# An attention kernel on one core: scores in runs of three half tiles, and each query block's context split inside the tile loop

## What is computed

```python
scores = jnp.einsum('bqhd,bkd->bhqk', q, k) * scale        # 16 heads, one k of width 32
scores = jnp.where(causal, scores, min_val)
attn = jax.nn.softmax(scores, axis=-1)
ctx = jnp.einsum('bhqk,bkd->bqhd', attn, v)
out = jnp.einsum('bsd,ed->bse', ctx, out_w) + out_b
x = layernorm(x + out)
```

## Time and profile before

| | us |
|---|---|
| median of 3 runs | 1208.55 |
| lowest and highest of them | 1206.21, 1215.7 |
| the profiled execution | 1208.3 |
| its span, first to last instruction | 1206.1 |

### The profile page before, as it was taken

How to read it: one execution, slowest core, us unless ns; L and a number is a source line. 1 busy time by engine, 2 the same in 40 slices (tenths; PEclk the granted TensorE clock), 3 DMA queues, 4 the chain that set the end, 5 groups by cost and what they waited for, 6 DMA issues and landing times.

```text
span 1206.1 us, 18310 instructions
## 1 busy us (share of the span) xinstructions
PE 1102.0 (91%) x6056; PEld 529.5 (44%) x6080; DVE 896.4 (74%) x1095; ACT 712.2 (59%) x828; POOL 165.5 (14%) x153
## 2 busy tenths in 40 slices
PE   5499989998999999999988998999999899999986
PEld 4146433743335543333643743374333464333342
DVE  3176688769987689888677668865988757988856
ACT  4344568337884477886435346824788446788711
POOL 4220121102001011001013012020200101100000
PEclk9699999999999999999999999999999999999989
DMA  9911530064001550001153154016300135000000
GB/s 214 235 55 34 120 93 2 36 141 105 1 1 36 118 129 1 2 1 36 34 134 94 39 126 106 2 36 141 105 2 1 36 81 131 1 1 2 2 1 36
DMA packets 65678, 74.37 MB, mean 62 GB/s; under 512 B 14224, under 2 KB 48016, under 8 KB 65552
## 3 DMA queue, kind: packets, MB, share of 16 engines
q1 hardware_dynamic: 49968, 58.74, 19.2%
q0 software_dynamic: 13584, 11.54, 6.1%
q10 hardware_dynamic: 2000, 2.51, 0.7%
HBM read 25.58 MB, written 8.39 MB: 28 GB/s over the span
## 4 chain that ended last, share of the span: by engine, by line
PE 58%; DVE 25%; issue 8%; ACT 2%; POOL 2%; SPq 2%; DVEq 1%; DMA 1%; ACTq 0%; POOLq 0%
DVE psum_k L743 14%; PE sc L1053 13%; PE bank L1075 11%; PE sc L943 10%; PE sc L1192 7%; PE bank L943 7%; PE sc L1207 2%; DVE stats L819 2%; PE sc L1093 2%; DVE res L816 2%; SPq L364 2%; ACT prob L577 2%; PE bank L1093 2%; PE sc L1138 1%; POOL prob L467 1%
## 5 line engine op out<-in xcount | busy, mean ns | idle before, releaser
L577 ACT ACTIVATE prob<-sc 128x1024 f32<-128x1024 f32 x544 | 525.2, 1026 | 156.7 <-PE sc L1053 142.8
L743 DVE TENSOR_TENSOR psum_k<-psum_k,prob 128x2048 f32<-128x2048 f32 x170 | 395.6, 2327 | 5.1
L1053 PE MATMUL sc<-q_st,k_st 128*128 128x512 f32 x1088 | 334.3, 428 | 32.2 <-DMA q_st<-q_lo 16.3
L1053 PEld LDWEIGHTS sc<-q_st,k_st 128*128 128x128 f32 x1088 | 186.5, 191 | 279.8 <-ACT prob L577 180.2
L1075 PE MATMUL bank<-prob,v_sb 128*32 128x512 f32 x2176 | 289.1, 607 | 0.8 <-DVE ctxn L802 0.8
L467 POOL TENSOR_SCALAR_AFFINE_SELECT prob<-prob 128x1024 f32<-128x1024 f32 x64 | 88.0, 1419 | 605.6 <-ACT prob L577 605.5
L1192 PE MATMUL sc<-prob,w_sb 128*128 128x512 bf16 x488 | 117.9, 381 | 5.3 <-DVE prob L892 2.9
L743 DVE TENSOR_TENSOR psum_k<-prob 128x2048 f32<-128x2048 f32 x28 | 64.1, 2288 | 52.8 <-ACT prob L577 43.9
L1075 PEld LDWEIGHTS bank<-prob,v_sb 128*32 128x32 f32 x2176 | 43.8, 108 | 106.8 <-issue 89.9
L943 PE MATMUL bank<-q_st,wq_hi 128*128 128x512 f32 x240 | 81.0, 402 | 0.0
L609 ACT ACTIVATE prob<-sc 128x512 f32<-128x512 f32 x64 | 37.3, 597 | 68.1 <-PE sc L1192 68.0
(11 more groups left out here) (127 smaller groups left out, 998.6 us busy)
## 6 DMA issues: line engine op xcount, KB each, us to landing
q_st<-q_hi SPq DMA_DIRECT2D x128, 128.0 KB, 2.8
q_st<-q_lo SPq DMA_DIRECT2D x128, 128.0 KB, 2.8
res<-in_x SPq DMA_DIRECT2D x8, 1024.0 KB, 5.2
res<-ob_sb POOLq DMA_DIRECT2D x8, 1024.0 KB, 10.1
out_x<-res SPq DMA_DIRECT2D x32, 256.0 KB, 5.6
res<-in_xT SPq DMA_DIRECT2D x7, 1024.0 KB, 5.0
w_sb<-in_w POOLq DMA_DIRECT2D x8, 256.0 KB, 14.3
prob<-in_wqkvT ACTq DMA_DIRECT2D x4, 288.0 KB, 5.9
```

Of the source, the lines that this page charges most:

```text
L577: nc.scalar.activation(prob[t % NP][:, half * HW:(half + 1) * HW], score_half(q // TB, 2 * t + half).rearrange("p m n -> p (m n)"), ACT.Ex ...
L743: nc.vector.tensor_tensor(acc[:, :], first[:, :], prob[t % NP][:, :], ALU.add).then_inc(add_v, 1)
L1053: last = nc.tensor.matmul(dst, k_st[:, k * P:(k + 1) * P], q_st[slot][:, c * HJ:(c + 1) * HJ, at:at + P], start=True, stop=not shift)
```

## The change

The halves of the scores are no longer issued two at a time, tile by tile. A group's first two halves stand alone; after that they come in runs of three. A run is followed by the values of each tile that it has completed, alternately one tile and two, and by the denominators due at those tiles. `scored_by(g, u)` gives the tiles complete after half u, and is empty in the middle of a run. The ring's list of uses (`ring_of`) has the same new order, so denominators always stand between two runs.

The splits of the context move: the high part of block q is made on ACT after the exponential of tile `LAST[q] + 6`, the low part on DVE at tile `LAST[q] + 8`, where these tiles still belong to the group; otherwise behind the last tile, where all but the fourth block's now stand ahead of `split_high_x`. The number of instructions of each kind is as before.

```diff
+HIGH_LAG, LOW_LAG = 3, 5
+def split_at(q, lag):
+    t = LAST[q] + DLAG + lag
+    return t if t <= LAST[q // TB * TB + TB - 1] else None
+
+def halves_of(g):
+    return range(2 * FIRST[TB * g], 2 * LAST[TB * g + TB - 1] + 2)
+
+def scored_by(g, u):
+    first, last = halves_of(g)[0], halves_of(g)[-1]
+    if u == first + 1:
+        return [u // 2]
+    if u != last and (u - first - 1) % 3:
+        return []
+    begin = first + 2 + 3 * ((u - first - 2) // 3)
+    return range((begin + 1) // 2 if begin % 2 == 0 else begin // 2, (u + 1) // 2)
+
 def ring_of(g):
     uses = []
-    for t in range(FIRST[TB * g], LAST[TB * g + TB - 1] + 1):
-        uses += [("scores", 2 * t), ("scores", 2 * t + 1)]
-        uses += [("den", q) for q in denominators_at(t) if q >= TB * g]
+    for u in halves_of(g):
+        uses.append(("scores", u))
+        uses += [("den", q) for t in scored_by(g, u) for q in denominators_at(t) if q >= TB * g]
...
                         exp_tile(t)
-                        if t == t1 - 1:
-                            split_high_context(g, 0)
-                    split_high_context(g, 1)
+                        for n in range(TB):
+                            if split_at(TB * g + n, HIGH_LAG) == t:
+                                split_high_context(g, n)
+                    for n in range(TB - 1):
+                        if split_at(TB * g + n, HIGH_LAG) is None:
+                            split_high_context(g, n)
                     with if_more(act, b, g):
                         split_high_x(g + 1)
-                    split_high_context(g, 2)
                     split_high_context(g, TB - 1)
...
-                        if t > t1 - 2:
-                            split_low_context(g, t - t1 + 1)
+                        for n in range(TB):
+                            if split_at(TB * g + n, LOW_LAG) == t:
+                                split_low_context(g, n)
...
-                    for t in range(t0, t1 + 1):
-                        scores(t, g, shift)
-                        if t == t0 and g:
+                    for u in halves_of(g):
+                        scores(u, g, shift)
+                        if u == 2 * t0 + 1 and g:
                             finish_experts(g - 1)
-                        if t - LAG >= t0:
-                            times_values(PV_ORDER[t - LAG])
-                        for q in denominators_at(t):
-                            if q >= TB * g:
-                                denominators(q)
+                        for t in scored_by(g, u):
+                            if t - LAG >= t0:
+                                times_values(PV_ORDER[t - LAG])
+                            for q in denominators_at(t):
+                                if q >= TB * g:
+                                    denominators(q)
```

More of the change, by code:

```diff
@@ L927, in _ @@
                                 normalise_context(q)
-                    split_low_context(g, 2)
+                    for n in range(TB - 1):
+                        if split_at(TB * g + n, LOW_LAG) is None:
+                            split_low_context(g, n)
                     normalise_context(TB * (g + 1) - 1)
@@ L1035, in ring_free, with scores @@
                             pe.wait_ge(rden_ready, count(b, rden_ready, i + 1))
-                def scores(t, g, shift):
+                def scores(u, g, shift):
+                    t, half = divmod(u, 2)
                     q, k = TILES[t]
                     slot, at = (q % TB) // 2, (q % 2) * P
[L1040 to L1061, removed]
@@ new lines, in scores @@
+                    at_ring = RING_AT[g]["scores", u]
+                    ring_free(g, at_ring)
+                    if at_ring == 2:
+                        with pe.If(b > 0) if g == 0 else nullcontext():
+                            pe.wait_ge(resid2, count(b - (g == 0), resid2, TB * ((g - 1) % NG) + (2 if g else TB)))
+                            pe.sem_inc(waited_apart, 1)
+                    for m in range(2):
+                        c = 2 * half + m
+                        if t == FIRST[q] and q % 2 == 0:
+                            pe.wait_ge(stack_in[slot][c], count(b, stack_in[slot][c], 64 * (g + 1)))
+                        dst = score_half(g, u)[:, m, :]
+                        last = nc.tensor.matmul(dst, k_st[:, k * P:(k + 1) * P],
+                                                q_st[slot][:, c * HJ:(c + 1) * HJ, at:at + P],
+                                                start=True, stop=not shift)
+                        for j in range(HJ if shift else 0):
+                            h = c * HJ + j
+                            last = nc.tensor.matmul(dst[:, j * P:(j + 1) * P],
+                                                    minus_max[:, q % TB, h:h + 1].broadcast_to([P, P]),
+                                                    ident[:, :], start=False, stop=(j == HJ - 1))
@@ L1063, in times_values @@
+                    last.then_inc(scored, 1)
                 def times_values(t):
```

## The result

| | median us | lowest to highest | runs |
|---|---|---|---|
| before | 1210.56 | 1198.53 to 1220.69 | 20 |
| changed | 1216.12 | 1210.13 to 1220.65 | 20 |

The ratio is 1.0045, 95% interval 1.0027 to 1.0064: slower, by some 5 us. I had forecast 1198 us, and so 10 us faster. The time stands within 1% of before, which was the likeliest of my three cases, and just within my range, but the sign is wrong and clear of the noise.

A forecast was written before the change was run, and what follows sets the result against it. PE was taken to set the pace, except where DVE comes late at group starts. Per sequence 0.3 + 2.4 + 2.1 (second to fourth groups) + 0.5 (ends) = 5.3 us, twice 10.6, from 1208.3: 1198 us, range 1186 to 1217.

The forecast's parts named there:

- my three cases: Whole kernel: faster by more than 1%, chance 0.37; within 1%, 0.52; slower by more than 1%, 0.11.
- What bounds the kernel: Late fourth group: PE sets the pace at 2.12 us a tile; at starts of groups two to four DVE does.
- the 0.32 us of the two changes of shape: Tile loop: PE loses 0.32 us of each tile's 2.12 going from scores to values and back.
- The strict reading of the Trainium skill: Scores to values: early weight loads make the change free, so runs win nothing; 1217 us, the no-gain rival's time, chance 0.13.
- Does ACT keep up?: Steady runs: three exponentials need 2.81 of 3.01 us, slot met by 0.2 to 0.4; no stall, gain 0.11 us a tile.
- The denominators: Third half behind denominators waits for DVE's transpose: stall 0.7 us (q = 4, 5), 1.0 or 0.1 (q = 0, 9, 12).
- the case of the buffer that the denominators must read first: q = 10, 13, 14: exponential waits until denominators have read the buffer it overwrites; stall 0.5 us.
- The starts of groups: DVE times fixed, only PE's work done by then changes: second group -0.4 us, third +0.9, fourth -0.85.
- noise either way: Clock falls to 1.2 GHz: moving PE's idle times may shift a few, 1.5 us each, either way; not priced.
- The splits: Moved into the loop on ACT, 11 times a sequence: 0.2 us of stall each, bounds 0 and 0.63; DVE nothing.
- the idle time of 2.48 us: Group's end: PE starts its projection 2.48 us behind the values, by no wait that the trace names.
- the ring that binds: Rival: each run's third half waits for ACT; at 0.34 us a run about 1247 us with the losses; chance 0.10.

The follow-up runs named there:

- the short exponentials: Full change with exponentials one eighth narrower (896 of 1024 columns) from a sequence's sixth tile; two runs late in the fourth group 6.03 us, profiled span 1199.3 us.
- two of my own kernels: Full change with pairs in the first group, ratio 1.014 to the kernel before; the same plus DVE's normalisation ahead of that tile's addition, ratio 0.9979.
- the kernel where it was 1.65 us: Full change, but the first group of a sequence keeps pairs of scores; ratio 1.014 to the kernel before, ends 81.2 us.

## Why the prediction was wrong

**What bounds the kernel: right.** PE sets the pace in the late loop, the 0.32 us of the two changes of shape are real, and the short exponentials give 6.03 us for three tiles as summed. The strict reading of the Trainium skill, TensorE: Matmul & The Clock Gate, in the table at its head, by which the changes would be free, is refuted by that.

**"Does ACT keep up?": the step that failed first.** I let runs follow each other every 3.01 us, and found 0.2 to 0.4 us to spare. 3.01 is a mean. Behind a run with one completed tile the next begins after 1.59 + 1.00 = 2.59 us, behind one with two after 3.44. In the short distance ACT's three exponentials, 2.81 us, don't fit, and the third half waits. The working on the denominators had two unlike distances, 2.47 and 3.33 us; the question on ACT was put to the mean alone. By my own numbers: the third exponential ends 3.67 us behind its run's start, 1.08 into a run that begins at 2.59, later than the 0.85 us at which its weights were due. The gain is 0.05 us a tile and not 0.11. On the 28 and 41 tiles of the third and fourth group this is 1.6 and 2.4 us a sequence, 8 of the 16 us that lie between forecast and result (an estimate, from the late pattern).

**The denominators: right in kind, too small in size.** The stalls stand where the working put them, behind q = 4, 5, 9 and 12, with the transpose as their end. Behind q = 8 I had written none, since a tile's values cover the wait; PE sits idle there for 2.00 us in mid run in the first sequence (303.71 below) and 1.17 in the second. The cover was reckoned with the DVE of the steady pattern too. For q = 9 I had 1.0 us and the trace has 1.7 and 2.9 in the two sequences. I had the DVE of the steady pattern there, and in the third group it is late: its first addition waits 2.03 us for a mask.

```profile
321.84 2.29 DVE L769 TENSOR_TENSOR psum_k<-prob 128x2048 f32<-128x2048 f32 x1 [2.03 <-POOL prob L491]
326.38 0.71 DVE L818 STREAM_TRANSPOSE rden<-sc 128x512 f32<-128x512 f32 x1
```

For q = 10, 13 and 14, the case of the buffer that the denominators must read first, I had 0.5 us. At q = 13 it is 0.41 before the run and 0.46 inside it, 0.9 together, since the slot wait comes twice:

```profile
505.97 0.73 PE L1081 MATMUL sc<-q_st,k_st 128*128 128x512 f32 x2 [0.36 <-ACT prob L601]
506.89 1.20 PE L1081 MATMUL sc<-q_st,k_st 128*128 128x512 f32 x4 [0.19 <-ACT prob L601]
```

**The starts of groups: right, and spoilt in one.** In the fourth group the third half waits until 43.7 us into the loop (473.06 - 429.35), where the scores of before stood at 43.5 (468.09 - 424.61), one tile's values behind, as written. In the third PE reaches DVE's transpose two halves ahead, as written, after 36.3 us (303.71 - 267.38) against 36.2 (299.35 - 263.18). But PE has then stood idle in mid run, and what it does next is slow:

```profile
303.71 0.73 PE L1081 MATMUL sc<-q_st,k_st 128*128 128x512 f32 x2 [2.00 <-DVE rden L818]
304.37 1.28 PE L1103 MATMUL bank<-prob,v_sb 128*32 128x512 f32 x8
305.58 2.93 PE L1081 MATMUL sc<-q_st,k_st 128*128 128x512 f32 x6
```

The six score matmuls behind it take 2.93 us and not 1.65: the granted clock is at 1.2 GHz there (0.54 in the mean from 304.8 to 308.2). In the second sequence the same happens behind q = 9, after an idle time of 2.71 us. This costs some 1.3 to 1.5 us in each sequence's third group. I had set the clock down as noise either way, and in number it is that: the kernel before has such a stretch in each second group, where four matmuls take 1.95 us behind the 2.19 us of idle time, and the changed kernel has none there, behind 2.50 us. The lower clock has moved from the second group to the third, which is a part of why the one gained more than forecast and the other lost.

By group, for the loops, mean of both sequences, forecast against measured: second 0.3 faster, 1.0 faster; third 2.4 faster, 2.0 slower; fourth 2.1 faster, 0.3 slower.

**The splits: inside the bounds, wrong in size.** I took 0.2 us for each, and the sum had 0.6 us in each of three groups, 3.6 us in all. Alone they cost nothing and bring up to 4 us; the lower bound of zero was the right value. In pairs ACT has 0.18 us a tile to spare and takes it. In the full change, where ACT has less, the seven loops are 1.9 us shorter with the splits moved than without (652.9 and 651.0). That is less than these loops repeat to, so no cost is seen there, and none can be ruled out.

**What I priced at nothing and was not nothing.** The first group's loop, 7.5 us in the profiled execution, by two transfers that meet differently. And the ends: I had named a lower clock as noise of 1.5 us each and taken the idle time of 2.48 us as fixed. It is not: the runs bring a second pause of 1.04 and 1.08 us in the fourth groups and shorten the pause of the first groups by 1.6 us each. In the profiled execution of the changed kernel the ends came out shorter than before, 68.0 against 74.4 us, mostly in the first groups, so they don't explain its loss; they do explain those of two of my own kernels.

**The rivals.** The one on the other side, the ring that binds, named the right mechanism, the third half that waits for ACT, and priced it at every run and 0.34 us. It is every second run and 0.17 us. With the denominators' stalls, and the first group's loop, that is enough to turn the sign.

## What to carry to other kernels

When work is bunched, check each distance in the new cycle against the consumer's time, not the mean distance: a ring of three slots has no room for a run of three behind a short gap. A wait placed in the middle of a bunch costs all the work that used to stand between producer and wait, so first ask what the releasing engine does just before it releases; here, moving DVE's transpose ahead of one addition was worth more than the bunching, and the bunching paid only away from it.

## What the runs showed of the hardware

An idle time that the trace mostly gives to no engine stands behind PE's jump over a long unused branch: 1.7 to 3.1 us in all kernels here, and 0.8 to 1.3 at the first groups' ends where the first group went in runs. Where the fourth group went in full runs, a second one of up to 1.9 us followed a few matmuls later, and in the kernel where it was 1.65 us the matmuls behind it ran at a granted clock of 1.2 GHz. The eight ends of groups took 66.8 to 85.3 us in thirteen kernels with the same work in them. A difference of half a percent between two versions of this kernel therefore says little without a look at the ends; the seven loops, which repeat within 3 us, say more.
